# Filler products of the identity in front of 25 waits of TensorE in a four-block attention kernel

## The reference, cut to what matters

```
L0: 16 heads over channels; attention mean and deviation; out = instance_norm(x) * std + mean
L1: 16 heads of width 16, keys from context and latents (256), then out_w, RMS norm, GELU MLP 256 -> 1024 -> 256
L2: LN, cross attention with 16 heads of width 128 -> residual; LN, a second one -> residual; LN, GELU MLP
L3: LN, cross attention with 16 heads of width 16, 128 keys -> residual; LN, GELU MLP
```

## Time and profile before

| | before |
|---|---|
| median of 3 runs | 1232.23 us |
| profiled execution, its own time | 1233.65 us |
| its span, first to last instruction | 1231.9 us |
| mean granted TensorE clock, of full speed | 0.952 |
| busy: PE / DVE / ACT / POOL | 1081.0 / 747.5 / 722.5 / 321.1 us |
| matmul records of TensorE | 8224 |

### The profile page before, as it was taken

One profiled execution on the slowest core, in us unless ns is written; L12 is line 12 of the kernel. 1 busy time (PEld: TensorE's weight loads), 2 busy tenths in 40 slices (PEclk: granted clock), 3 DMA queues, 4 the chain that ended last, 5 costly groups with the idle time before them and its releaser, 6 DMA issues. The chain is left out here.

```text
span 1231.9 us, 23777 instructions
## 1 busy us (share of the span) xinstructions
PE 1081.0 (88%) x8224; PEld 952.6 (77%) x8224; DVE 747.5 (61%) x1763; ACT 722.5 (59%) x2096; POOL 321.1 (26%) x433
## 2 busy tenths in 40 slices
PE   3799995899968899999999989999999687789687
PEld 2577773777748878999999869999998587667487
DVE  4777674687876545555555745555555756666753
ACT  1577774778774346566656556656665433688631
POOL 5234335455440003111111112111111111343210
PEclk9799997999998999999999989999999899899799
DMA  6111110000002111010111111111100111000101
GB/s 198 24 29 44 44 28 34 2 2 1 1 19 75 44 45 40 30 35 34 40 44 65 44 43 44 44 44 44 44 35 19 35 35 35 1 2 2 35 1 35
DMA packets 20364, 43.65 MB, mean 35 GB/s; under 512 B 3347, under 2 KB 10773, under 8 KB 20246
## 3 DMA queue, kind: packets, MB, share of 16 engines
q1 hardware_dynamic: 20246, 42.12, 10.4%
HBM read 36.87 MB, written 1.05 MB: 31 GB/s over the span
## 5 line engine op out<-in xcount | busy, mean ns | idle before, releaser
L1629 POOL TENSOR_TENSOR pt<-pt,prec 128x256 f32<-128x256 f32 (+1 forms) x224 | 180.3, 805 | 647.2 <-DVE prec L1467 513.7
L618 PE MATMUL ps<-rs 128*128 128x256 f32 x480 | 147.0, 306 | 29.5 <-DVE rs L1502 19.4
L1127 ACT ACTIVATE pt<-ps,nmax 128x129 f32<-128x129 f32 x256 | 92.4, 367 | 96.1 <-DVE nmax L1459 95.4
L1266 DVE TENSOR_TENSOR rs<-wraw,rs 128x256 fp32r<-128x256 f32 (+2 forms) x108 | 69.3, 644 | 121.9 <-ACT rs L1004 121.2
L620 PE MATMUL ps<-rs 128*128 128x256 f32 x480 | 139.0, 290 | 0.0
L619 PE MATMUL ps<-rs 128*128 128x256 f32 x480 | 139.0, 290 | 0.0
L618 PE MATMUL ps<-ht,rs 128*128 128x256 f32 (+1 forms) x368 | 128.1, 348 | 2.1 <-ACT rs L1055 1.1
L1078 ACT ACTIVATE pt<-ps,nmax 128x256 f32<-128x256 f32 (+1 forms) x256 | 105.2, 423 | 33.8 <-DVE nmax L1405 25.4
L618 PEld LDWEIGHTS ps<-rs 128*128 128x128 f32 x480 | 95.2, 198 | 35.8 <-DVE rs L1502 12.7
L619 PE MATMUL ps<-ht,rs 128*128 128x256 f32 (+1 forms) x368 | 122.0, 331 | 0.0
L620 PE MATMUL ps<-ht,rs 128*128 128x256 f32 (+1 forms) x368 | 121.5, 330 | 0.0
(11 more groups left out here) (198 smaller groups left out, 2989.9 us busy)
## 6 DMA issues: line engine op xcount, KB each, us to landing
wraw<-in_packs SPq DMA_DIRECT2D x55, 512.0 KB, 3.5
bvr<-in_l2rows SPq DMA_DIRECT2D x16, 256.0 KB, 4.6
rs<-rs SPq DMA_DIRECT2D x80, 32.0 KB, 1.9
ht<-rs SPq DMA_DIRECT2D x48, 32.0 KB, 1.9
row<-in_rows SPq DMA_DIRECT2D x2, 640.0 KB, 5.1
out<-X SPq DMA_DIRECT2D x1, 1024.0 KB, 4.5
X<-in_x SPq DMA_DIRECT2D x1, 768.0 KB, 7.5
XH<-in_ctx SPq DMA_DIRECT2D x1, 768.0 KB, 9.3
```

What stands on the lines that cost most here:

```text
L618: nc.tensor.matmul(dst, w[0], m[1], start=start, stop=False)
L1127: last = nc.scalar.activation(prob[:, g % 3, k * D:k * D + P + 1], ps[:, S_BANK + g % 2, k * D:k * D + P + 1], ACT.Exp, bias=nmax[:, g % 4 ...
L1266: last = nc.vector.tensor_tensor(dst[1], src, f32(dst[0]), ALU.subtract)
L1629: nc.gpsimd.tensor_tensor(pr, pr, prec[:, u % 4, 0:nh].unsqueeze(2).broadcast_to([P, nh, keys]), ALU.mult)\
```

## The change

A table `FILL` gives 25 steps a number, 220 in sum. A new function `fill` is called at the head of `norm_step`, of `PV` and `WO` in `att`, and of `down` in `mlp`, ahead of all waits of the step. It issues that many products of the identity with itself, float32, 128x128 by 128x128, into the first 128 columns of PSUM bank 0. Nothing reads them, nothing waits for them and they signal nothing.

```diff
+FILL = {("lat", 0): 28, ("lat", 2): 3, ("lat", 3): 6, ("PV", "L1", 31): 12, ("WO", "L1", 3): 6, ("L1r", 2): 5, ("L1r", 3): 5,
+        ("L2n1", 3): 6, ("L2n2", 2): 5, ("L2n2", 3): 5, ("L2nm", 0): 12, ("L2nm", 2): 6, ("L2nm", 3): 5,
+        ("down", "L2", 0): 14, ("L3n1", 2): 28, ("L3n1", 3): 5, ("PV", "L3", 30): 6, ("PV", "L3", 31): 8, ("WO", "L3", 3): 6,
+        ("L3nm", 2): 6, ("L3nm", 3): 6, ("down", "L3", 0): 13,
+        ("down", "L1", 3): 8, ("down", "L2", 3): 8, ("down", "L3", 3): 8}
...
+            def fill(*at):
+
+                for _ in range(FILL.get(at, 0)):
+                    nc.tensor.matmul(ps[:, S_BANK, 0:P], ident[:, :], ident[:, :], start=True, stop=True)
+
             def norm_step(e, name, k):
 
                 if e != "nT":
                     return
                 n = N[name]
+                fill(name, k)
                 bank = j_bank()
...
                 elif e == "PV":
+                    fill("PV", ph, i)
                     it, r = divmod(i, 2 * STEPS)
...
                 elif e == "WO":
+                    fill("WO", ph, i)
                     pe.wait_ge(a["oeD"], i + 1)
...
                 elif e[0] == "down":
                     c = e[1]
+                    fill("down", name, c)
                     if c == 0:
```

## The result

The changed kernel takes 1218.76 us in the median of 4 runs (1216.34 to 1220.79), the kernel before 1232.18 us beside it (4 runs): a ratio of 0.989, 95% interval 0.9869 to 0.9911, or 13.4 us less. Forecast were 1217 us and 1209 to 1226 us. The profiled execution took 1216.34 us, the shortest of the four, where the one of before, 1233.65 us, was 1.5 us above its median; so the two traces lie 17.4 us apart, 4 us more than the medians. 1.6 us of that are won ahead of the first filler, before anything differs between the kernels.

What follows compares the result with a forecast made beforehand. TensorE, busy 88% of the span, was taken as the spine, losing time to waits and its low clock. Gains of 3.0 + 2.4 + 1.5 + 2.7 + 1.5 + 1.5 + 2.8 = 15.4 us gave 1217 us, range 1209 to 1226.

Steps and rivals of the forecast that it cites:

- The price of a filler: Each filler product takes 0.22 us of TensorE at the high clock, 0.43 us at the low one.
- `lat`, 3.0 us: `lat` transposes: third and fourth step gain 0.4 us each, dense products behind them 2.2 us; sum 3.0 us.
- `L2n2`, 2.7 us: Before L2's second attention: step 3 gains 0.4 us, TensorE's chain to 720.71 us takes 2.35 instead of 4.7.
- `L2n1`, nothing: Step 3, 6 fillers: next two `v` steps get 1.7 us shorter, but the third waits for DVE; no gain.
- `L2nm`, nothing: 12, 6 and 5 fillers gain nothing, since DVE is busy without a gap from there to `down` 0.
- `L3nm`, nothing: 6 and 6 fillers in L3 gain nothing, since DVE covers the steps.
- `L3n1` 2 late at no cost: 28 fillers end 2.0 us after the 4.17 us wait, but the next step waits for DVE anyway; no cost.
- the bound of 29 us: Largest possible gain, half of 58.23 us, if all TensorE work at the low clock were on the chain.
- `down` 3 and `down` 0, 1.5 and 1.4: `down` 3 of L1 and `down` 0 of L2 gain 1.5 us each, `down` 0 of L3 gains 1.4.
- `L3n1` 3 to L3's attention, 1.5 us: Step 3 of `L3n1` gains 0.4 us and the dense step behind it 1.1; sum 1.5 us.
- Given back at the waits without filler: Rival: longer unfilled waits bring new low stretches, 5 to 8 us given back, say 1224 us; chance 0.22.
- Slower: Rival: fillers run at the low clock, 0.43 us each, and cost 19 us together, 1251 us; chance 0.06.

Runs made afterwards that it cites:

- the kernel with the 163: Changed kernel without the fillers at the eight places forecast to gain nothing, 163 of the 220 left: 1219.61 us.
- the kernel with the filled start: Changed kernel plus 55 products of a loaded weight ahead of five waits at the start of L0: 1219.97 us.
- the last kernel: Changed kernel plus 31 products in L2's wide attentions, POOL's two clears cut in eight, and 10 instead of 28 fillers at `L3n1` 2: 1214.16 us.

## Why the prediction was right

The mechanism came out: the gain lies where work at the low clock sits on TensorE's chain, and is nothing where DVE covers it. The size came out as well, 15.4 us forecast, 15.7 us between the two traces from `lat` 3 on and 15.6 us in the second profile of the changed kernel, but that close only by luck. Two terms were 2.3 us too large together, and low stretches that the sum did not hold gave 2.1 us back. And the three traces flatter it: before's lies 1.5 us above its median, those of the changed kernel 2.4 and 1.2 us below theirs. Point by point:

- *The price of a filler*, 0.22 us from the score products of the earlier trace rows, is what the fills take (0.223 us from start to start).
- *`lat`, 3.0 us*: 1.95 measured. The two steps that DVE releases are 0.4 us shorter each, but neither was on the chain: the third and the fourth stand 2.86 us apart in both traces, since DVE comes to its split of k = 1 only after work of its own, and the products behind the fourth start 0.75 us after it, against 0.77. The dense products won 1.9 of their 2.2 us, up to 218.85 us of the trace of before. The late start of the clock, 8.05 us for 28 products, was foreseen, and it cost nothing: the `lat` steps stand as far apart as before.
- *`L2n2`, 2.7 us*: 1.5 measured, in both profiles of the changed kernel. That TensorE alone is the chain from 716.0 to 720.71 us was wrong: with the clock up it waits there, 0.45 us of it for DVE's split (L1331). The other 1.0 us up to T 66 comes from the low stretch at 730.95 us of before, behind the unfilled wait at T 64. I had not counted it, and it did not come again, though nothing was put there. That is not certain: the kernel with the 163 has it again, and wins nothing from T 64 to T 66.
- *`L2n1`, nothing; `L2nm`, nothing; `L3nm`, nothing; `L3n1` 2 late at no cost*: right to 0.02 us in the two stretches that hold `L2n1` and `L3n1`; the one with `L2nm` won 0.4 us, at the end of the last pass, ahead of any of its fillers, and uncounted too. Such places keep the gain below the bound of 29 us: the work at the low clock there got shorter as elsewhere, and the wait behind it longer, as the 1.89 us at `v` 2 shows.
- *`down` 3 and `down` 0, 1.5 and 1.4*: right.
- *`L3n1` 3 to L3's attention, 1.5 us*: 2.3 measured, 1.6 of them ahead of 1065 us in the trace of before. The rest is the low stretch behind L3's first scores there, which did not come again; I had not counted it.
- *The median*, 1217: 1218.76 and 1219.9 measured, so the gain in the medians is 12 to 13 us, not 15. Part of the rest is the choice of the profiled executions, as said above; no profile of a slower execution shows what is left. *Given back at the waits without filler* is seen in single profiles: one of the kernel with the filled start has a low stretch at 384 us, behind the uncovered wait at `down` 0 of L1, and wins 1.0 us from L1's first `dv` to `down` 3 where the changed kernel wins 2.5. The kernels with half and with half more of each count have one behind `v` 2 of L2, the wait that the prediction had named, and lose 1.5 us there. DVE's long copy costs 1.5 us in four of thirteen profiles, but in none of the two of the changed kernel. How often each strikes in the changed kernel was not measured.
- *The rule of the Trainium skill* ("TensorE: Matmul & The Clock Gate", What's actually happening) that the ramp costs under 1% of a typical span: 13.4 us are 1.1%, and the last kernel is 17.8 us below the one before beside it (1231.96 us), of which by the traces 3 to 4.5 are DVE's. Right in order of size, a little low.
- *Slower*: its condition, fills at the low clock or beyond the wait, does not hold in the changed kernel; its price does hold, as the kernels with half more and with the fills behind the waits show.

## What to carry to other kernels

Ahead of a wait of TensorE, products that nobody reads are free as long as they end before it, and where they keep the clock up, the work behind the wait gets shorter (12 products in 1.69 us instead of 2.93). That shortens the kernel only if that work is on the chain. So price each place by what its next long stretch waits for, count the fill from the wait's length at the high clock, and rather stay a fifth below it, as here at `PV` 31: half too many lost nearly as much as half too few. A sum of places can come out right while its terms do not, so compare it place by place. And look at what a longest wait is made of: here one had a POOL clear in it, worth 3.1 us in the trace, more than any single fill.

## What the hardware showed that I had not expected

- A DVE copy of 128x2 elements, issued while POOL clears 128x4096, takes 2.49 us or 5.94 us, against 0.17 us where POOL clears nothing: it ends with the POOL instruction that runs, or with the next one. With clears of 128x512 it takes 0.43 us.
- Transposes of the identity held TensorE's mean granted clock at 0.982 to 0.988 in four executions, as products did (0.981 to 0.990 in nine).
- Half of the fill was enough at waits of 2.1 us and of 3.5 us (`down` 3 of L1, `down` 0 of L2), and not at `PV` 31 of L1 with the same 3.5 us.
